# The 48 left-over rows of an expert's down product as two products of 64 rows on the halves of TensorE's array

## The reference, cut to what matters

```python
logits = xt @ Ws + bs                              # 8 experts
topk_w, topk_idx = top_k(logits, 2); topk_w = softmax(topk_w)
combine = sum(one_hot(topk_idx, E) * topk_w[..., None], axis=1)
g = einsum('td,edf->tef', xt, Wg)                  # F = 688
u = einsum('td,edf->tef', xt, Wu)
h = silu(g) * u
y = einsum('tef,efd->ted', h, Wd)
out = einsum('ted,te->td', y, combine)
```

## Time and profile before

| what | value |
|---|---|
| median of 3 runs | 665.9 us (665.02 to 666.17) |
| the profiled execution: time | 662.45 us |
| its span, first to last instruction | 660.5 us |
| mean granted TensorE clock | 0.987 |
| PE busy | 619.4 us, 94% of the span |
| VectorE, ScalarE, POOL busy | 372.0, 314.8, 293.1 us |
| L804 (gate and up) | 1408 instructions, 164.6 us |
| L853 (down) | 384 instructions, 88.5 us |

### The profile page before, as it was taken

The page is one execution under the profiler, slowest core; times in us unless marked ns, Lnnn a source line. Parts: engine busy times, 40 slices in busy tenths (PEclk is TensorE's granted clock), DMA queues, the critical chain, the costliest instruction groups (busy, mean ns, idle before and its releaser), DMA issues.

```text
span 660.5 us, 16877 instructions
## 1 busy us (share of the span) xinstructions
PE 619.4 (94%) x5901; PEld 526.5 (80%) x5902; DVE 372.0 (56%) x995; ACT 314.8 (48%) x813; POOL 293.1 (44%) x524
## 2 busy tenths in 40 slices
PE   6999976999999998999899979999999999999995
PEld 5999963677777776777677768999999999999984
DVE  2677885777777876788777858322222222222245
ACT  2455452777777775777667675112122211221214
POOL 3535464343364359334863351434334242525244
PEclk9999997999999999999999999999999999999998
DMA  8333215566665644543343248777676776766443
GB/s 245 117 85 80 60 37 158 136 187 196 197 191 182 191 128 127 143 118 102 113 113 99 77 147 285 263 241 220 224 231 227 222 214 199 214 213 228 142 132 139
DMA packets 72898, 109.37 MB, mean 166 GB/s; under 512 B 9786, under 2 KB 50562, under 8 KB 72066
## 3 DMA queue, kind: packets, MB, share of 16 engines
q1 hardware_dynamic: 66882, 100.40, 48.9%
q0 software_dynamic: 5952, 8.14, 5.4%
HBM read 73.77 MB, written 12.44 MB: 131 GB/s over the span
## 4 chain that ended last, share of the span: by engine, by line
PE 51%; DMA 18%; issue 8%; DVE 7%; POOL 6%; POOLq 6%; ACT 2%; SPq 1%; DVEq 0%; ACTq 0%
DMA accd<-y,si 16%; PE ps L1593 7%; PE ps L1645 6%; PE ps L1667 6%; PE ps L1620 5%; PE ps L1604 5%; POOLq L726 5%; PE ps L804 4%; PE ps L1688 2%; PE ps L1653 2%; PE ps L1524 2%; PE ps L853 2%; DMA xT_sb<-in_xT 2%; PE ps L1513 1%; PE ps L1532 1%
## 5 line engine op out<-in xcount | busy, mean ns | idle before, releaser
L2138 DVE TENSOR_REDUCE cmx<-ps 100x1 f32<-100x361 f32 x256 | 134.6, 532 | 66.6 <-PE ps L1593 62.3
L804 PE MATMUL ps<-xsT,W 128*128 128x128 f32 x1408 | 164.6, 275 | 1.5 <-DVE hT L994 1.5
L804 PEld LDWEIGHTS ps<-xsT,W 128*128 128x128 f32 x1408 | 160.5, 192 | 2.2 <-DVE hT L994 1.9
L1913 ACT ACTIVATE cpr<-ps 128x300 f32<-128x300 f32 x256 | 104.9, 420 | 58.3 <-PE ps L1604 57.0
L853 PE MATMUL ps<-WD,hT 128*128 x384 | 88.5, 380 | 2.4 <-DVE hT L997 1.8
L1593 PE MATMUL ps<-st 96*100 96x361 bf16 x256 | 85.7, 338 | 5.2 <-DVE cmx L2138 2.3
L1604 PEld LDWEIGHTS ps<-st 120*128 120x128 bf16 x768 | 62.6, 102 | 32.7 <-issue 9.4
L1604 PE MATMUL ps<-st 120*128 120x100 bf16 x768 | 76.6, 208 | 4.4 <-ACT st L1918 2.0
L853 PEld LDWEIGHTS ps<-WD,hT 128*128 128x128 f32 x384 | 70.5, 190 | 11.3 <-issue 3.1
L1008 DVE TENSOR_SCALAR y<-ps,wt 128x256 f32<-128x256 f32 x28 | 13.5, 484 | 106.3 <-PE ps L853 106.3
L720 POOL DMA_INDIRECT accd<-y,si x28 | 45.0, 1605 | 64.1 <-DMA accd<-y,si 54.9
(11 more groups left out here) (267 smaller groups left out, 1020.5 us busy)
## 6 DMA issues: line engine op xcount, KB each, us to landing
W<-in_wgu SPq DMA_DIRECT2D x32, 1408.0 KB, 6.4
st<-parts SPq DMA_DIRECT2D x192, 115.2 KB, 2.5
WD<-in_wd SPq DMA_DIRECT2D x6, 1024.0 KB, 5.7
cx<-in_ctxT SPq DMA_DIRECT2D x16, 361.0 KB, 3.9
x_sb<-in_x SPq DMA_DIRECT2D x8, 200.0 KB
x1d<-x SPq DMA_DIRECT2D x8, 200.0 KB
x1Td<-x1T SPq DMA_DIRECT2D x8, 200.0 KB, 3.4
x1T_sb<-x1Td SPq DMA_DIRECT2D x16, 100.0 KB, 3.4
```

What stands on the lines that cost most here:

```text
L804: mm = pe.matmul(out[:, i * P:(i + 1) * P], self.columns(t, k, c), self.xsT[:, t.par, k, :], start=(k == 0), stop=(k == KC - 1))
L1913: act.activation(pr[:, h % (2 * HG), :], ps[:, B_T + h % 2, 0:NCH * L], ACT.Exp).then_inc(exp_ok, 1)
L2138: dve.tensor_reduce(mx[:, half, hh:hh + 1], ps[0:L, B_S + h % 2, 0:CTX], AX_X, ALU.max).then_inc(max_ok, 1)
```

## The change

For the 28 early tiles the sixth product, of 128 rows (48 of them used) and 256 columns, gives way to two products of 64 rows and 128 columns: rows 0 to 63 give columns 0 to 127 and add to the bank of the other chunks, rows 64 to 127 give columns 128 to 255 in a bank of their own (`B_Z`). For that the 48 rows of `hT` are written twice, at partitions 0 and 64. `WD`'s sixth chunk is laid out by the host with the first half of the columns at partitions 0 to 47 and the second at 64 to 111, zeros elsewhere, so that the late tiles' full product still gives the same sum. VectorE copies the two halves of it for a tile's expert to `wl` two tiles ahead (`stage`), and for tiles 0 and 1 in the last iteration of the attention, at h = 10. `weigh` gets a second operation that adds bank Z, scaled, to columns 128 to 255 of `y`, behind a wait for the first one; `y_ok` counts two for each early tile (`weighed`). PE waits for the last logits before the loop, since bank 1 was in use before.

```diff
--- before.py
+++ after.py
@@ -484,6 +484,11 @@
         eng.wait_ge(sem, count)
 
 
+def weighed(n):
+
+    return 2 * n if not isinstance(n, int) else 2 * min(n, LT) + max(n - LT, 0)
+
+
 def stand(eng, waits_met):
 
 
@@ -553,7 +558,7 @@
 
 
     B_C, B_Y, B_G, B_U, B_X = 2, 3, 4, 5, 6
-    B_ROUTE = 0
+    B_ROUTE, B_Z = 0, 1
     N_CONST = 6
     GAT_OK, EXPERTS_OK, SCA_OK = 14, 15, 17
     DOWN_IN = {TILES - 3: 6, TILES - 1: 4}
@@ -615,6 +620,7 @@
         self.sg = sb("sg", [P, 6 * P])
         self.wt = sb("wt", [P, 4, E])
         self.hT = sb("hT", [P, 2, FC, P])
+        self.wl = sb("wl", [P, 2, P])
         self.y = sb("y", [P, 2, D])
         self.acc = sb("acc", [P, TP + 1, D])
         self.stats = sb("fstats", [P, TP + 1, 6])
@@ -715,7 +721,7 @@
             pool.tensor_copy(self.si[:, t.par:t.par + 1].bitcast(I32), self.sca[:, bass.ds(t.n, 1)]).then_inc(self.si_ok, 1)
             pool.wait_ge(self.si_ok, t.n + 1)
             wait(pool, self.added, 16 * t.n)
-            pool.wait_ge(self.y_ok, t.n + 1)
+            pool.wait_ge(self.y_ok, weighed(t.n + 1))
             stand(pool, self.pool_stands)
             pool.indirect_dma_start(self.accd, bass.IndirectOffsetOnAxis(ap=self.si[:, t.par:t.par + 1], axis=0),
                                     self.y[:, t.par, :], None, compute_op=ALU.add, bounds_check=last_token,
@@ -838,20 +844,25 @@
         pe.matmul(self.ps[0:1, self.B_ROUTE, n:2 * n], self.R.ev16[0:VT, :], self.sel[:, :], start=True, stop=True)\
             .then_inc(self.route_mm, 1)
 
-    def tensor(self, pe):
+    def tensor(self, pe, logits_read):
         R, ps, hT, WD = self.R, self.ps, self.hT, self.WD
         pe.wait_ge(self.const, self.N_CONST)
         pe.wait_ge(R.wd_in, 16 * FC)
         pe.wait_ge(R.split_ok, 10)
-
-        def down(t, bank, freed):
+        pe.wait_ge(logits_read, NB)
+
+        def down(t, bank, freed, late):
             e = pe.value_load(self.expert_of[0:1, bass.ds(t.n, 1)], min_val=0, max_val=E - 1)
             if bank == self.B_Y:
-                wait(pe, self.y_ok, freed)
+                wait(pe, self.y_ok, weighed(freed))
             pe.wait_ge(self.h_ok, 2 * t.n + 2)
-            for c in range(FC):
+            for c in range(FC if late else FULL):
                 mm = pe.matmul(ps[:, bank, 0:D], hT[:, t.par, c, :], WD[:, c, bass.ds(e, 1), :],
                                start=(c == 0), stop=(c == FC - 1))
+            if not late:
+                pe.matmul(ps[:, bank, 0:P], hT[0:U_AT, t.par, FULL, :], self.wl[0:U_AT, t.par, :], start=False, stop=True)
+                mm = pe.matmul(ps[:, self.B_Z, 0:P], hT[U_AT:P, t.par, FULL, :], self.wl[U_AT:P, t.par, :],
+                               start=True, stop=True)
             mm.then_inc(self.y_mm, 1)
 
         def emit(t, n):
@@ -859,7 +870,7 @@
                 self.gate_up(pe, t + 1, 0, 0, 4)
             if n == 5:
                 pe.wait_ge(self.routed, self.EXPERTS_OK)
-            down(t - 1, self.DOWN_IN.get(n - 1, self.B_Y), t.n - 1 if n < TILES - 1 else TILES - 3)
+            down(t - 1, self.DOWN_IN.get(n - 1, self.B_Y), t.n - 1 if n < TILES - 1 else TILES - 3, n > LT)
             if n + 2 < TILES:
                 self.turn_rows(pe, t + 2)
             if n + 1 < TILES:
@@ -873,7 +884,7 @@
     def rows_out(self, act, t, bank=B_X):
         act.wait_ge(self.xT_mm, t.n + 1)
         wait(act, self.gu_mm, 3 * (t.n - 1))
-        wait(act, self.y_ok, t.n - 3)
+        wait(act, self.y_ok, weighed(t.n - 3))
         act.activation(self.wt[:, t.slot, :], self.xs[:, t.slot, D:XW], ACT.Copy)
         act.activation(self.xsT[:, t.par, :, :], self.ps[:, bank, 0:KC * P].rearrange("p (k t) -> p k t", k=KC),
                        ACT.Copy).then_inc(self.xT_ev, 1)
@@ -982,6 +993,12 @@
                                  op1=ALU.add).then_inc(routed, 1)
         dve.wait_ge(routed, self.EXPERTS_OK)
 
+    def stage(self, dve, t):
+        e = dve.value_load(self.expert_of[0:1, bass.ds(t.n, 1)], min_val=0, max_val=E - 1)
+        wait(dve, self.y_mm, t.n - 1)
+        for rows, half in ((slice(0, U_AT), slice(0, P)), (slice(U_AT, P), slice(P, D))):
+            dve.tensor_copy(self.wl[rows, t.par, :].unsqueeze(1), self.WD[rows, FULL, bass.ds(e, 1), half])
+
     def hidden(self, dve, t, part):
         dve.wait_ge(self.sg_ok, 2 * t.n + (2 if part == 1 else 1))
         dve.wait_ge(self.gu_mm, 3 * t.n + part + 1)
@@ -991,7 +1008,9 @@
             wait(dve, self.y_mm, t.n - 1)
             left = slice(U_AT, U_AT + FLEFT)
             dve.tensor_tensor(self.hT[:, t.par, FULL - 1, :], self.sg[:, 4 * P:5 * P], self.ps[:, self.B_C, 2 * P:3 * P], ALU.mult)
-            h = dve.tensor_tensor(self.hT[left, t.par, FULL, :], self.sg[left, 5 * P:6 * P],
+            dve.tensor_tensor(self.hT[left, t.par, FULL, :], self.sg[left, 5 * P:6 * P], self.ps[left, self.B_C, P:2 * P],
+                              ALU.mult)
+            h = dve.tensor_tensor(self.hT[0:FLEFT, t.par, FULL, :], self.sg[left, 5 * P:6 * P],
                                   self.ps[left, self.B_C, P:2 * P], ALU.mult)
         else:
             h = dve.tensor_tensor(self.hT[:, t.par, 0:FULL - 1, :].rearrange("p c t -> p (c t)"), self.sg[:, 0:4 * P],
@@ -1007,6 +1026,10 @@
             wait(dve, self.added, 16 * (t.n - 1))
             dve.tensor_scalar(self.y[:, t.par, :], self.ps[:, self.B_Y, 0:D], self.wt[:, t.slot, bass.ds(e, 1)], None,
                               ALU.mult).then_inc(self.y_ok, 1)
+            dve.wait_ge(self.y_ok, 2 * t.n + 1)
+            dve.scalar_tensor_tensor(out=self.y[:, t.par, P:D], in0=self.ps[:, self.B_Z, 0:P],
+                                     scalar=self.wt[:, t.slot, bass.ds(e, 1)], in1=self.y[:, t.par, P:D], op0=ALU.mult,
+                                     op1=ALU.add).then_inc(self.y_ok, 1)
 
         def weigh_late(t):
             q = t.n - LT
@@ -1018,7 +1041,7 @@
                                      op1=ALU.add).then_inc(self.y_ok, 1)
 
         def late_moments(q):
-            dve.wait_ge(self.y_ok, LT + q + 1)
+            dve.wait_ge(self.y_ok, weighed(LT + q + 1))
             dve.bn_stats(self.lstats[:, q, :], lat[:, q, :]).then_inc(self.mv_ok, 1)
             dve.wait_ge(self.mv_ok, self.at["late stats", q])
             dve.bn_aggr(self.lmv[:, q, :], self.lstats[:, q, :]).then_inc(self.mv_ok, 1)
@@ -1064,6 +1087,8 @@
         def emit(t, n):
             if n <= LT:
                 weigh(t - 1)
+                if n + 1 < LT:
+                    self.stage(dve, t + 1)
             if n == LT + 1:
                 sums_of(0)
                 sums_of(1)
@@ -1851,7 +1876,7 @@
                 mm.then_inc(X.route_mm, 1)
                 X.gate_up(pe, Step(0, 2), 0, 2, 4)
                 X.pack(pe)
-                X.tensor(pe)
+                X.tensor(pe, lg_ev)
 
             @block.scalar
             def _(act):
@@ -2260,6 +2285,10 @@
                                 R.chosen(dve, 3)
                                 R.which(dve, 3)
                                 R.total(dve, 3)
+                            if h == 10:
+                                dve.wait_ge(R.wd_in, 16 * FC)
+                                X.stage(dve, Step(0, 0))
+                                X.stage(dve, Step(0, 1))
                             if h == 11:
                                 R.scaled(dve, 3, ps[0:L, B_O, 0:(GROUPS[3][1] - GROUPS[3][0]) * E])
                                 R.place(dve, 3)
@@ -2377,7 +2406,8 @@
 
         w = np.zeros((E, FP, D), d.dtype)
         w[:, 0:FULL * P, :] = d[:, 0:FULL * P, :]
-        w[:, FULL * P + U_AT:FULL * P + U_AT + FLEFT, :] = d[:, FULL * P:, :]
+        for at, half in ((0, slice(0, P)), (U_AT, slice(P, D))):
+            w[:, FULL * P + at:FULL * P + at + FLEFT, half] = d[:, FULL * P:, half]
         return w
 
 
```

## The result

The changed kernel takes 674.6 us, the median of 8 runs; the kernel before, beside it, 666.2 us: 8.5 us slower. One of the 8 runs was a slow one of 1583 us; the other seven (671.8 to 676.1) have a median of 674.2, and their ratio to the kernel before is 1.0117 with a 95% interval of 1.0092 to 1.0141, which is 7.8 us (6.1 to 9.4). The forecast was 670.2, with a range up to 673.6: the direction was right, and the 4.3 us were half of what came. The profiled execution of the changed kernel took 674.24 us, with a span of 672.3, against 662.45 and 660.5 before.

The account below looks back on a forecast made before the run. PE's pace in the experts' steps was taken as the bound, up to the last weight load, then scatters in a row. 3.6 us (steps) + 0.7 (first stagings) = 4.3 on the 665.9 median gave 670.2; range 667.4 to 673.6.

Parts of the forecast that it names:

- What bounds the kernel: Experts' stretch: PE, busy throughout its 7.72 us step, sets the pace of weight loads and scatters; last y has 2.3 us spare.
- The left-over product: Down product of each early tile: two half passes side by side take 0.22 us instead of 0.43, gaining 0.21.
- Going into halves and back: Both ends of the half products: empty 0.09 plus an open weight load each, together 0.35 us; step grows 0.14 to 7.86.
- only the gaps count: Ends of the halves: weight loads stay hidden, price 0.18 us, step shrinks 0.03; as a rival 665.8 us, chance 0.06.
- the passes of a half in one piece: Half products: both passes of one half go before the other's, one more pass of 0.11 shows, step grows 0.25.
- How many of them count: Steps before the weight load at 614.94: 26 of 28 shortened products count, 26 x 0.14 = 3.6 us.
- VectorE in the step: VectorE's added second weighing, staging and second write of 48 rows fit into its idle time in each step: cost nothing.
- The first two stagings: VectorE's queue before batch 15's moments: L2174 1.1 us late, x and PE's idle time 0.7 more; bounds 0 and 1.4.
- the later pass: Half products in each step: one more pass shows, step grows 0.25, giving 673.1 us; chance 0.07.
- free halves: Rival: entering and leaving the halves costs nothing, 5.5 us gained in the steps and 0.7 lost, 661.1 us; chance 0.09.
- a pair not taken in turns: Rival: PE finishes one half's passes before the other's, 673.1 us, chance 0.07; no overlap at all, 676.2, chance 0.03.
- scatters with a pace of their own: Rival: only what exceeds the last y's spare 2.3 us counts, 2.0 plus 0.7, giving 668.6 us; chance 0.08.

Follow-up runs that it names:

- two visits: Changed kernel with its first two stagings moved earlier; PE does one half after the third down chunk, the other at the end: 690.23 us, ratio 1.0324.
- two pairs: Changed kernel with its first two stagings moved earlier; the pair of half products done twice in each visit, the second time into unread columns: 674.55 us, ratio 1.0116.

## Why the prediction was right and wrong

- **What bounds the kernel**: right, for the steps. The two kernels that only lengthen PE's step (two visits, two pairs) come out later as a whole, and the one that adds only VectorE's work doesn't grow in its steps. In the two longer ones the last scatter waits for y (POOL idles 4.39 and 1.84 us before it), so the scatters keep up with such steps.
- **The left-over product**: right. In the kernel with two pairs, further passes start 0.11 us apart, each for both halves: 0.22 us in place of 0.43, 0.21 gained.
- **Going into halves and back**: right, in size too: 0.09 + 0.11 + 0.09 + 0.05 = 0.34 by the rows, 0.35 by the step. The step was forecast at 7.86 and is 7.861 us. The two bounds beside it (only the gaps count; the passes of a half in one piece) are both out: the trace shows the loads in the open and the passes by turns.
- **How many of them count**: close. y 27 is 3.81 us later by the steps, and the last scatters catch up 0.8, of which some 0.3 may be chance, so 3.0 to 3.3 of it reach the load of accd, where the sum had 3.6.
- **VectorE in the step**: right: nothing. Its own room was also as costed (0.46 us left, forecast some 0.3, since a copy takes 0.22 and not up to 0.29).
- **The first two stagings**: this is the step that failed, first by its size and then, in the next point, by what it left out. In it I wrote "L2174 is 1.1 us late" and "x is 0.7 late". By the trace the moments are 2.3 late and x 1.86. I put a value load at 0.52 us, by the sum of its rows in a quiet queue, begun as the residual starts and so nearly hidden behind it. It did begin there, at 402.4, but its own row was 0.56 us, not the 0.30 of the median, and it was 1.34 us from its start to the first copy; the second began only at 403.9, when the first copies had started, and took 0.74 to its own. So VectorE idled 0.97 and 0.45 us before copies of 0.46 each: 2.34 us in a row behind the residual, where I had 1.1. The slack of 0.44 ahead of x was read rightly: 2.3 - 0.44 is the 1.86 by which x came late. But that is over my bound of 1.4.
- **Missing from the sum**: that PE's idle time has a price beyond itself. I costed "PE idles 0.7 more" at 0.7. It idled 1.87 more, and behind that wait the clock fell, for another 3.1 us (x to y 0 is 18.44 in place of the 15.35 of the kernel with earlier stagings). This is the larger part of the miss. The two together are 5.0 in the trace, and 4.0 by the medians or 4.5 by the ratios of these two kernels, where the sum had 0.7. The range let none of this in: its upper end holds the later pass (673.1), a matter of the halves, and I read the wait of 0.80 ahead of L1695 as a duration only, and didn't ask what PE's clock would do if it grew. None of the three signs by which the prediction called itself wrong came true (a step under 7.72, L997 waiting for VectorE, the last scatters waiting for y), since they look at the steps and the scatters. The one that did show it was PE's idle time before the transposes of x: 2.67 us, where near 1.5 was forecast.
- **The rivals**: free halves and hidden loads are excluded by the step of 7.861; a pair not taken in turns by the timeline; scatters with a pace of their own by the 0.8 us that they catch up, which is less than the 2.3 that y had to spare. 673.1 and 676.2, the times of the third, lie near the measured one by accident: neither of their mechanisms is in the trace.

## What to carry to other kernels

In this kernel two products on halves of TensorE's rows ran side by side at the price of one, but a visit to the halves cost 0.35 us in and out, here more than the 0.21 us that one pair saves: count how many pairs one visit can take before you split a product. When work is put into a queue on the path between two stages, read the operation's time from its start to its first user, not as a sum of its parts, and ask how long PE will then stand idle: here the wait cost less (1.9 us) than the clock behind it (3 us). Look for a place in the same queue where that engine waits anyway: with the two stagings moved there, no stretch of the trace behind the residual shows them any more.

## What the runs showed of the hardware

- Before the transposes of x TensorE's clock fell behind a wait of 2.67 us (2.68 in the kernel with the stagings alone), and in the profiled executions not behind 1.34 or 0.80. In both kernels the granted clock then stood at 1.2 GHz for 6.8 us, although PE was busy in 96 and 89% of that time. PE's waits in the late tiles fit: it fell behind 2.93 and 3.17 us, behind 2.10 in the changed kernel but not behind the same 2.10 in two others, and not behind 2.00 or less. So the length of the wait alone doesn't decide at about 2 us. The Trainium skill, TensorE: Matmul & The Clock Gate, Part 1, has the array's clock halved when the engine has been idle; by that rule, the traces agree.
- Entering the halves and leaving them each cost an empty 0.09 us and then a weight load with nothing over it (0.11 us for 128 columns of f32, some 0.05 ahead of the transposes). Between pairs of the same split nothing is lost. The Trainium skill, TensorEngine Tiling (Array Packing), Key Properties, has the engine drain when the tiling mode changes; the empty 0.09 us are that drain as these traces show it, and the bare load comes on top.
- A value read into a register on VectorE and used as an address cost 0.74 to 1.34 us from the start of the load to the first copy, and for 0.97, 0.54 and 0.45 us of that the engine was idle. The sum of the rows that the queue shows for it is 0.52.
